# Cross-attention scores relative to the last key: 76 instead of 77 columns a head, heads interleaved key by key

## The chip, the cores and the metric

One core of one Trainium2 chip runs the whole kernel. The metric is the device time of one execution in microseconds, as the median of several runs.

## What is computed

A gated cross-attention layer with a linear layer behind it, over x of shape 4 x 2048 x 512 and a context of 4 x 77 x 384 (77 keys for each of 4 batches), with 16 heads of 64:

```
x = x + tanh(g_xattn) * attention(layernorm(x), ctx)
x = x + tanh(g_ffn) * (layernorm(x) @ W[idx] + b[idx])

q, k, v = xn @ Wq, ctx @ Wk, ctx @ Wv            # split into 16 heads of 64
sim  = einsum('bhid,bhjd->bhij', q, k) * 64**-0.5
attn = softmax(sim, axis=-1)                     # over the 77 keys j
out  = einsum('bhij,bhjd->bhid', attn, v) @ Wo + bo
```

A softmax doesn't change when the same number is taken from all scores of a row.

## The kernel before

**Folding.** Queries are never formed. In a first part (some 90 us) the kernel multiplies the projected keys by the turned Wq and the projected values by Wo, so that the scores of a row are x times a folded matrix, and the attention output is the probabilities times a folded matrix. `key_fold` makes the folded keys in 32 units (4 blocks of 128 features by 8 pairs of heads): two fp32 matmuls of B*J = 308 columns into a pair of PSUM banks. Each unit is then split into two f16 halves, high and low, in `a_split`: ScalarE casts the high half out of PSUM (`key_high`, L824), VectorE subtracts it for the low half (`key_low`, L1070). Seven units (`STAGED_KEYS`) take another way: ScalarE copies them to `k_stage` (L822), and GpSimd makes both halves from there (`key_split`, L660 and L662). `pair_of_heads` says where a unit's heads lie in `a_split`. Units of folded values, visited in turn with them (`VISITS`), go the same way through L811 and L1062. PSUM pairs are used in a round of four, so a matmul waits until the unit four places before it is out (`taken_before`).

**Projection.** `keys_of` (L1394) projects the keys: 24 fp32 matmuls of 308 columns from `ctxT`, the turned context that ScalarE copied out of PSUM (L741).

**Tiles.** Then 64 tiles of 128 rows of x run in a software pipeline; a loop body holds 8 tiles. For each tile TensorE issues:

- `scores` (L1355): 36 f16 matmuls. The 16 heads are laid into three PSUM banks of 6, 6 and 4 heads, of 462, 462 and 308 columns; each bank takes 4 blocks of features by 3 products (high x high, high x low, low x high), so 12 matmuls.
- products of the second layer (L1355 with 256 columns): 42 for two tiles.
- `attention` (L1355 with 512 columns, L1579): 29 matmuls for the tile before.

`s_bank` gives the bank: the scores rotate through banks 0 to 3, three a tile, and wait for the exponentials of the bank's last user. Behind the scores VectorE takes the maxima by head (`maxima`, L1151 and L1153), ScalarE 16 exponentials of 77 elements (`exponentials`, L858), VectorE multiplies by the reciprocal sums (L1162), ScalarE and VectorE split the probabilities into f16 halves (L873, L875, L425), SyncE issues their transposes by DMA (L564), and `attention` reads those in the next step. VectorE and ScalarE work strictly in the order of their `step` functions.

The first scores wait for the last folded units: `bank_folded(0)` for the low halves up to unit 29 (the last that used banks 0 and 1), `heads_folded(0)`, ahead of the last feature block of the first bank, for the staged units up to number 27.

## Time and profile before

| what | value |
|---|---|
| median of 3 runs | 1051.0 us (1050.85 to 1053.32) |
| profiled execution | 1052.3 us, span of its instructions 1050.5 us |
| TensorE matmul busy | 1034.4 us, 98% of the span |
| VectorE busy | 851.6 us, 81% |
| ScalarE busy | 743.7 us, 71% |
| GpSimd busy | 438.9 us, 42% |
| TensorE granted clock | 0.998 of full speed |

The span is from the first to the last instruction of the profiled execution. Busy time counts an engine's own work and not its waits; the chain that ended last is followed back from the last instruction, each time to what released it.

### The profile page before, as it was taken

To read this page: it belongs to the slowest core of one execution; us is meant where nothing else is said; L and a number is where in the kernel's file an instruction comes from. 1 tells how busy PE (TensorE), PEld (TensorE's weight loads), DVE (VectorE), ACT (ScalarE), POOL (GpSimd) and SP (SyncE) were. 2 spreads that over 40 slices of the span, in tenths; PEclk is the share of its full clock that TensorE was granted. 3 is DMA by queue.
4 is the path that set the end of the run, shared out by engine and by line. 5 is a ranking of instruction groups with operands and counts; after the bars stand their busy time and mean duration, and the time that the engine had idled before them with its cause. 6 is when DMAs were issued, how large, how long until landed. Compare 5 with 4: busy or idle time off the path is not lost.

```text
span 1050.5 us, 21819 instructions
## 1 busy us (share of the span) xinstructions
PE 1034.4 (98%) x6065; PEld 588.0 (56%) x6065; DVE 851.6 (81%) x1800; ACT 743.7 (71%) x2712; POOL 438.9 (42%) x635
## 2 busy tenths in 40 slices
PE   9998899999999999999999999999999999999998
PEld 7634455555555555555555555555555555555555
DVE  3867988888888887888888887888888887888876
ACT  3588887766776676767776677767776776767762
POOL 0575444444433343444433443444433443444322
PEclk9999999999999999999999999999999999999999
DMA  8413466656666656655666656655666656655655
GB/s 310 101 30 105 94 128 136 134 114 118 129 136 135 135 126 136 135 118 110 132 138 135 135 121 139 137 112 111 132 138 137 136 123 134 134 113 114 133 116 141
DMA packets 383639, 135.02 MB, mean 129 GB/s; under 512 B 361728, under 2 KB 363316, under 8 KB 383540
## 3 DMA queue, kind: packets, MB, share of 16 engines
q1 hardware_dynamic: 383476, 134.09, 59.0%
q14 instruction: 84, 0.69, 0.2%
q8 instruction: 15, 0.25, 0.1%
q0 software_dynamic: 64, 0.00, 0.0%
HBM read 27.48 MB, written 16.78 MB: 42 GB/s over the span
## 4 chain that ended last, share of the span: by engine, by line
PE 93%; DVE 3%; ACT 1%; DMA 1%; issue 1%; SPq 0%; POOL 0%; DVEq 0%
PE banks L1355 84%; PE banks L1579 3%; PE banks L1458 1%; PE banks L1385 1%; PE banks L1394 1%; PE banks L1466 1%; DVE vw_area L1062 1%; ACT vw_area L811 1%; PE banks L1447 1%; DMA fold_area<-in_ctx 1%; DMA work<-work 0%; ACT work L858 0%; DVE fold_area L1070 0%; DVE work L425 0%; DVE red L1153 0%
## 5 line engine op out<-in xcount | busy, mean ns | idle before, releaser
L858 ACT ACTIVATE work<-banks,red,cst 128x77 f32<-128x77 f32 x1024 | 409.1, 426 | 89.1 <-DVE red L1153 89.1
L1355 PE MATMUL banks<-fold_area,work 128*128 128x462 f16 (+1 forms) x2304 | 410.6, 336 | 1.4 <-DMA work<-work 0.7
L1355 PE MATMUL banks<-vw_area,work 128*128 128x512 f16 x1674 | 373.0, 380 | 2.6 <-DMA work<-work 2.6
L1355 PEld LDWEIGHTS banks<-fold_area,work 128*128 128x128 f16 x2304 | 223.9, 97 | 176.2 <-DMA work<-work 1.2
L1355 PEld LDWEIGHTS banks<-vw_area,work 128*128 128x128 f16 x1674 | 164.1, 98 | 188.4 <-DMA work<-work 2.9
L425 DVE SCALAR_TENSOR_TENSOR work<-work 128x256 f16<-128x256 f32 (+3 forms) x444 | 240.1, 575 | 3.8 <-ACT work L881 3.3
L858 ACT ACTIVATION_READ_ACCUMULATOR work<-banks,red,cst 128x1 f32 x1024 | 221.0, 216 | 0.0
L1151 DVE TENSOR_REDUCE stats<-banks 128x6 f32<-128x462 f32 (+1 forms) x192 | 112.0, 584 | 109.1 <-PE banks L1355 108.7
L1355 PE MATMUL banks<-work 128*128 128x256 f16 x1302 | 162.4, 272 | 1.6 <-DVE work L1236 1.6
L1355 PEld LDWEIGHTS banks<-work 128*128 128x128 f16 x1302 | 126.8, 98 | 33.1 <-DVE work L1236 2.2
L703 POOL TENSOR_TENSOR stats<-stats,cst 128x1 f32<-128x1 f32 x64 | 12.5, 195 | 283.8 <-DVE stats L1187 283.8
L873 ACT ACTIVATE work<-work 128x768 f16<-128x768 f32 (+1 forms) x128 | 82.0, 641 | 59.5 <-DVE work L1162 59.5
L624 POOL TENSOR_TENSOR stats<-stats,cst 128x1 f32<-128x1 f32 x64 | 50.1, 783 | 170.5 <-DVE stats L1006 170.5
L761 ACT ACTIVATE work<-work,stats 128x512 f32<-128x512 f32 x64 | 52.1, 814 | 94.0 <-POOL stats L629 79.1
L1162 DVE TENSOR_TENSOR work<-work,cst 128x924 f32<-128x924 f32 (+1 forms) x128 | 113.9, 890 | 4.4
L1236 DVE SCALAR_TENSOR_TENSOR work<-banks,cst,work 128x256 f32<-128x256 f32 x217 | 98.1, 475 | 22.6 <-issue 18.5
L727 POOL TENSOR_TENSOR work<-work 128x512 f32<-128x512 f32 x64 | 95.4, 1491 | 43.8 <-DVE work L1196 34.3
L881 ACT ACTIVATE work<-work 128x512 f16<-128x512 f32 x124 | 71.4, 576 | 9.6 <-DMA work<-work 5.9
L1153 DVE TENSOR_SCALAR red<-stats,cst 128x6 f32<-128x6 f32 (+1 forms) x192 | 60.8, 317 | 6.8
L1180 DVE SCALAR_TENSOR_TENSOR work<-banks,cst,work 128x512 f32<-128x512 f32 x64 | 47.6, 744 | 4.7 <-PE banks L1579 4.5
L721 POOL TENSOR_TENSOR work<-work 128x256 f32<-128x256 f32 x31 | 46.2, 1489 | 2.4
L1183 DVE BATCH_NORM_STATS2 stats<-work 128x6 f32<-128x512 f32 x64 | 44.5, 695 | 2.2
(145 smaller groups left out, 814.4 us busy)
## 6 DMA issues: line engine op xcount, KB each, us to landing
work<-in_x SPq DMA_DIRECT2D x64, 256.0 KB, 2.8
out<-work SPq DMA_DIRECT2D x63, 256.0 KB, 2.2
work<-work SPq DMA_TRANSPOSE x254, 3.1
fold_area<-in_L_xattn_Wo SPq DMA_DIRECT2D x4, 512.0 KB, 9.2
work<-in_L_ffn_W SPq DMA_DIRECT2D x2, 1024.0 KB, 7.0
fold_area<-in_L_xattn_Wq SPq DMA_DIRECT2D x2, 1024.0 KB, 12.9
fold_area<-in_L_xattn_Wk SPq DMA_DIRECT2D x2, 768.0 KB, 12.1
fold_area<-in_L_xattn_Wv SPq DMA_DIRECT2D x2, 384.0 KB, 6.8
```

What stands on the lines that cost most here:

```text
L425: return nc.vector.scalar_tensor_tensor(out=lo, in0=value, scalar=scale, in1=hi, op0=ALU.mult, op1=ALU.subtract)
L624: nc.gpsimd.tensor_tensor(ve1, mv1[:, 1:2], eps, ALU.add).then_inc(ve1_ready, 1)
L727: nc.gpsimd.tensor_tensor(xr[:, m2, :], xr[:, m2, :], bias, ALU.add).then_inc(x2b_ready, 1)
L761: nc.scalar.activation(xn_place(o1, m1), xr[:, m1, :], ACT.Identity, bias=nm1, scale=rstd1).then_inc(xn_ready, 1)
L858: nc.scalar.activation(probs_of(h, h + 1), s_bank(m, k)[:, (h - h0) * J:(h - h0 + 1) * J], ACT.Exp, bias=nmx[:, h:h + 1], scale=exp_scale, ...
L873: nc.scalar.activation(by_core(ps[:, h0 * CORE:h1 * CORE]), values[:, :, 0:CORE], ACT.Copy, scale=2.0 ** PROB_BITS).then_inc(p_hi, 1)
L881: nc.scalar.activation(group_stage(g)[:, 0, :], value, ACT.Copy, scale=2.0 ** XN_BITS).then_inc(x2_hi, 1)
L1151: nc.vector.reduce_max(mx[:, h0:h1], by_head(s_bank(m, k)), AX.X).then_inc(mx_ready, 1)
L1153: nc.vector.tensor_scalar(nmx[:, h0:h1], mx[:, h0:h1], nexp_scale, None, ALU.mult).then_inc(nmx_ready, 1)
L1162: nc.vector.tensor_tensor(values, values, factors.unsqueeze(2).to_broadcast([P, h1 - h0, J]), ALU.mult).then_inc(p_ready, 1)
L1236: nc.vector.scalar_tensor_tensor(out=half, in0=part, scalar=f_scale, in1=half, op0=ALU.mult, op1=ALU.add).then_inc(f_added, 1)
L1355: mm = nc.tensor.matmul(ps, lhs(l), rhs(r), start=first and n == 0, stop=last and n == 2, skip_group_check=onto)
```

## The change

The last key is made the zero of the scores. Four GpSimd subtractions (one per batch) make `ctxT_from_last`, the turned context of keys 0 to 75 less that of key 76; `keys_of` reads it, so projected and folded keys have 76 columns a batch and head (304 for 308), and a score is that of its key less that of the last. The values still use all 77 keys. In a bank of scores the columns are laid key by key, the bank's heads side by side: column j*6 + h (j*4 + h in the bank of four heads, which starts at column 152, so that all banks end at 456). TensorE writes 456 and 304 columns, in one stretch. Columns 456 to 461 of banks 0 to 3 stand for the last key: VectorE sets them to zero once, and TensorE never writes them again, since score matmuls end in front of them. The maxima and the exponentials read 77 elements of a head through `s_heads`, 6 (or 4) fp32 elements apart. `a_split` has the same order, so the fold writes f16 elements 6 (or 4) places apart.

```diff
+    JS = J - 1
+    HS = HEADS * JS
+    BS = B * JS
...
-        a_split = [fold_area[:, k * A_WORDS:(k + 1) * A_WORDS].bitcast(F16).rearrange("p (s b n) -> p s b n", s=2, b=B) for k in range(KT)]
+        a_split = [fold_area[:, k * A_WORDS:k * A_WORDS + B * HS].bitcast(F16).rearrange("p (s b n) -> p s b n", s=2, b=B) for k in range(KT)]
...
         def s_bank(m, k):
             h0, h1 = BANKS[k]
-            return banks[:, (3 * m + k) % S_BANKS, 0:(h1 - h0) * J]
+            return banks[:, (3 * m + k) % S_BANKS, HB * JS - (h1 - h0) * JS:HB * JS]
+        def s_heads(m, k):
+            h0, h1 = BANKS[k]
+            cols = banks[:, (3 * m + k) % S_BANKS, HB * JS - (h1 - h0) * JS:HB * JS + h1 - h0]
+            return cols.rearrange("p (j h) -> p h j", h=h1 - h0)
...
         def pair_of_heads(k, s, h):
             four, a = h // 2, h % 2
-            cols = a_split[k][:, s, :, 4 * four * J:4 * (four + 1) * J].rearrange("p b (e r j) -> p e b r j", e=2, r=2)
-            return cols[:, :, :, a, :]
+            cols = a_split[k][:, s]
+            if four == 1:
+                at, apart = HB - 2 + a, HB * JS - (HB - 2)
+                return cols[:, :, at:at + 2 * apart].rearrange("p b (e n) -> p e b n", e=2)[:, :, :, 0:HB * (JS - 1) + 1:HB]
+            n = (0, None, 1, 2)[four]
+            h0, h1 = BANKS[n]
+            pairs = cols[:, :, h0 * JS:h1 * JS].rearrange("p b (j i r) -> p i b r j", i=(h1 - h0) // 2, r=2)
+            first = (4 * four - h0) // 2
+            return pairs[:, first:first + 2, :, a, :]
...
+            for b in range(B):
+                keys = ctxT[:, :, b * J:(b + 1) * J]
+                pool.wait_ge(ctxT_copied, b + 1)
+                nc.gpsimd.tensor_tensor(ctxT_from_last[:, :, b * JS:(b + 1) * JS], keys[:, :, 0:JS], keys[:, :, JS:J].to_broadcast([P, CT, JS]),
+                                        ALU.subtract).then_inc(ctxT_shifted, 1)
...
-                    nc.scalar.activation(probs_of(h, h + 1), s_bank(m, k)[:, (h - h0) * J:(h - h0 + 1) * J], ACT.Exp,
+                    nc.scalar.activation(probs_of(h, h + 1), s_heads(m, k)[:, h - h0, :], ACT.Exp,
                                          bias=nmx[:, h:h + 1], scale=exp_scale, accum_out=sums[:, h:h + 1]).then_inc(exp_done, 1)
...
+                if (kind, n) == (KEY, UNITS - 3):
+                    assert all(pair_of(KEY, v) >= S_BANKS for v in (UNITS - 2, UNITS - 1))
+                    dve.wait_ge(k_staged, key_staged_before(UNITS))
+                    dve.wait_ge(a_lo, key_highs_after(UNITS - 3))
+                    nc.vector.memset(banks[:, 0:S_BANKS, HB * JS:HB * J], 0.0).then_inc(last_zeroed, 1)
...
-                nc.vector.reduce_max(mx[:, h0:h1], by_head(s_bank(m, k)), AX.X).then_inc(mx_ready, 1)
+                nc.vector.reduce_max(mx[:, h0:h1], s_heads(m, k), AX.X).then_inc(mx_ready, 1)
...
+                if h == 0:
+                    pe.wait_ge(ctxT_shifted, B)
...
                 for n, (h0, h1) in enumerate(BANKS):
+                    if is_tile(o, m, 0) and n == 0:
+                        pe.wait_ge(last_zeroed, 1)
...
                         mm = split_products(s_bank(m, n), lambda s: turned[:, s, k, :],
-                                            lambda s: a_split[k][:, s, m % B, h0 * J:h1 * J], k == LAST_FOLDED[0], k == LAST_FOLDED[-1])
+                                            lambda s: a_split[k][:, s, m % B, h0 * JS:h1 * JS], k == LAST_FOLDED[0], k == LAST_FOLDED[-1])
```

In `copy_k`, `key_high`, `pair_banks`, `keys_of` and `key_fold` the width 0:BJ becomes 0:BS; `kT` and `k_stage` shrink with it.

VectorE, at the end of the fold and into the first tile (L1070 in before, L1097 in the change, are the low halves of key units; names are output<-input tiles). Before:

```order
L1002 BN_STATS stats<-work 128x6
L1006 BN_AGGR stats<-stats 128x2
L1070 TENSOR_TENSOR fold_area<-banks,fold_area 128x2x4x77 x6
L425 SCALAR_TENSOR_TENSOR work<-work 128x512
L1151 TENSOR_REDUCE stats<-banks 128x6
```

The same place in the change:

```order
L1029 BN_STATS stats<-work 128x6
L1033 BN_AGGR stats<-stats 128x2
L1097 TENSOR_TENSOR fold_area<-banks,fold_area 128x2x4x76 x4
L1170 MEMSET banks 128x4x6
L1097 TENSOR_TENSOR fold_area<-banks,fold_area 128x2x4x76 x2
L446 SCALAR_TENSOR_TENSOR work<-work 128x512
L1183 TENSOR_REDUCE stats<-banks 128x6
```

The memset stands between the low halves of units 29 and 30; nothing else moved.

GpSimd, at its start (constants, then the zeroed pads of the value side, then the first value split). Before:

```order
L618 MEMSET cst 128x1
L631 MEMSET vw_area 128x32x8
L637 CAST vw_area<-work 128x4x208
```

In the change:

```order
L639 MEMSET cst 128x1
L655 TENSOR_TENSOR fold_area<-fold_area 128x3x76 x4
L658 MEMSET vw_area 128x32x8
L664 CAST vw_area<-work 128x4x208
```

The four subtractions stand ahead of the pads. TensorE's instructions keep their order and number; its score matmuls read 128x456 and 128x304 for 128x462 and 128x308.

## Rows read from the trace of the kernel before

**Rows 1.** The page: span, busy time, and the chain by engine.

```profile
span 1050.5 us, 21819 instructions
PE 1034.4 (98%) x6065; PEld 588.0 (56%) x6065; DVE 851.6 (81%) x1800; ACT 743.7 (71%) x2712; POOL 438.9 (42%) x635
...
PE 93%; DVE 3%; ACT 1%; DMA 1%; issue 1%; SPq 0%; POOL 0%; DVEq 0%
```

**Rows 2.** Busy time by stretch: PE, PEld, DVE, ACT, POOL, clock, DMA share, GB/s.

```profile
48.00:79.00 31.00, 28.16 (x199) 11.63 (x197) 21.59 (x30) 25.35 (x35) 23.97 (x25) 1.00 0.24 44
110.00:1020.00 910.00, 906.65 (x5238) 510.91 (x5236) 754.34 (x1629) 661.33 (x2529) 373.79 (x549) 1.00 0.61 128
```

**Rows 3.** The chain of waits in order of time: start, us, what.

```profile
23.15 3.11 PE banks L1394 x12
...
90.44 2.51 PE banks L1355 x12
...
115.54 4.90 DMA work<-work
...
184.43 14.70 PE banks L1355 x87
...
214.05 14.70 PE banks L1355 x87
...
1028.96 0.76 DVE work L1180
```

**Rows 4.** Groups by line and shape: busy us, mean ns, idle before.

```profile
L1355 PE MATMUL banks<-vw_area,work 128*128 128x512 f16 x1674 | 373.0, 380 | 2.6 <-DMA work<-work 2.6
L1355 PE MATMUL banks<-fold_area,work 128*128 128x462 f16 x1536 | 310.3, 358 | 1.4 <-DMA work<-work 0.7 <-issue 0.7
L1355 PE MATMUL banks<-fold_area,work 128*128 128x308 f16 x768 | 110.8, 294 | 0.0
L1151 DVE TENSOR_REDUCE stats<-banks 128x6 f32<-128x462 f32 x128 | 81.5, 637 | 96.8 <-PE banks L1355 96.4
L1151 DVE TENSOR_REDUCE stats<-banks 128x4 f32<-128x308 f32 x64 | 30.6, 478 | 12.3 <-PE banks L1355 12.3
L1070 DVE TENSOR_TENSOR fold_area<-banks,fold_area 128x616 f16<-128x616 f32 x25 | 19.0, 794 | 4.5 <-ACT fold_area L824 4.4
L824 ACT CAST fold_area<-banks 128x616 f16<-128x616 f32 x25 | 16.4, 688 | 0.7 <-PE banks L1466 0.7
L1062 DVE TENSOR_TENSOR vw_area<-banks,vw_area 128x1024 f16<-128x1024 f32 x11 | 13.4, 1222 | 7.4 <-ACT vw_area L811 7.4
L811 ACT CAST vw_area<-banks 128x1024 f16<-128x1024 f32 x11 | 11.1, 1012 | 4.6 <-PE banks L1458 4.5
L1153 DVE TENSOR_SCALAR red<-stats,cst 128x6 f32<-128x6 f32 x128 | 31.1, 243 | 4.5
L716 POOL TENSOR_TENSOR work<-work 128x256 f32<-128x256 f32 x31 | 37.5, 1210 | 2.4
```

**Rows 5.** Timeline: the start, and the end of the fold.

```profile
8.41 0.35 ACT L741 COPY fold_area<-banks 128x231 f32<-128x231 f32 x1 [1.22 <-PE banks L1375]
...
35.58 0.88 POOL L637 CAST vw_area<-work 128x832 f16<-128x832 f32 x1 [32.00 <-ACT work L795]
...
87.42 4.33 DVE L1070 TENSOR_TENSOR fold_area<-banks,fold_area 128x616 f16<-128x616 f32 x6
...
89.41 0.70 POOL L660 CAST fold_area<-work 128x616 f16<-128x616 f32 x1
90.19 1.31 POOL L662 TENSOR_TENSOR fold_area<-work,fold_area 128x616 f16<-128x616 f32 x1
90.44 12.67 PE L1355 MATMUL banks<-fold_area,work 128*128 128x462 f16 x72 [0.67 <-issue]
```

**Rows 6.** Timeline of one tile in the middle.

```profile
510.55 3.09 SPq L564 DMA_TRANSPOSE work<-work  x1
...
518.96 5.99 PE L1355 MATMUL banks<-vw_area,work 128*128 128x512 f16 x27
```

More of the change, by code:

```diff
@@ L93, in flamingo_layer @@
         ctxT = c.take(CT * BJ).rearrange("p (k n) -> p k n", k=CT)
+        ctxT_from_last = c.take(CT * BS).rearrange("p (k n) -> p k n", k=CT)
         assert c.at <= 3 * A_WORDS
@@ L153, in flamingo_layer @@
         c.at = folds
-        kT = c.take(HP * BJ).rearrange("p (h n) -> p h n", h=HP)
+        kT = c.take(HP * BS).rearrange("p (h n) -> p h n", h=HP)
         wqT = c.take(HP * D).rearrange("p (h n) -> p h n", h=HP)
-        k_stage = [c.take(2 * BJ).rearrange("p (e n) -> p e n", e=2),
-                   at(D + HP * BJ, 2 * BJ).rearrange("p (e n) -> p e n", e=2)]
-        assert c.at <= x2T_at and D + HP * BJ + 2 * BJ <= RING * D
+        k_stage = [c.take(2 * BS).rearrange("p (e n) -> p e n", e=2),
+                   at(D + HP * BJ, 2 * BS).rearrange("p (e n) -> p e n", e=2)]
+        assert c.at <= x2T_at and D + HP * BJ + 2 * BS <= RING * D
         free = x2T_at + KT * D
@@ L204, in flamingo_layer @@
             sem("ident_zero"), sem("ident_ready"), sem("floor_set"), sem("consts_set"), sem("pads_set"))
-        ctxT_done, ctxT_copied = sem("ctxT_done"), sem("ctxT_copied")
+        ctxT_done, ctxT_copied, ctxT_shifted = sem("ctxT_done"), sem("ctxT_copied"), sem("ctxT_shifted")
         v_done, v_copied, v_scaled, v_scaled_end = sem("v_done"), sem("v_copied"), sem("v_scaled"), sem("v_scaled_end")
@@ L231, in flamingo_layer @@
         s_done, mx_ready, nmx_ready, exp_done = sem("s_done"), sem("mx_ready"), sem("nmx_ready"), sem("exp_done")
+        last_zeroed = sem("last_zeroed")
         rsum_ready, p_ready, p_hi, p_lo, pT_turned, pad_zeroed = (
@@ L393, in pair_banks @@
         def pair_banks(first):
-            return banks[:, first:first + 2, 0:BJ].rearrange("p e (b j) -> p e b j", b=B)
+            return banks[:, first:first + 2, 0:BS].rearrange("p e (b j) -> p e b j", b=B)
         def pair_of_stage(stage):
@@ L777, in copy_k @@
                 nc.scalar.copy(kT[:, 2 * n:2 * n + 2, :],
-                               banks[:, pair_of(PROJECT, n):pair_of(PROJECT, n) + 2, 0:BJ]).then_inc(k_copied, 1)
+                               banks[:, pair_of(PROJECT, n):pair_of(PROJECT, n) + 2, 0:BS]).then_inc(k_copied, 1)
             copy_k(0)
@@ L821, in key_high @@
                         act.wait_ge(k_stage_lo, n - 1)
-                    nc.scalar.copy(k_stage[n % 2], banks[:, first:first + 2, 0:BJ]).then_inc(k_staged, 1)
+                    nc.scalar.copy(k_stage[n % 2], banks[:, first:first + 2, 0:BS]).then_inc(k_staged, 1)
                 else:
@@ L1393, in keys_of @@
                 for k in range(CT):
-                    mm = nc.tensor.matmul(banks[:, pair_of(PROJECT, h // 2) + h % 2, 0:BJ], wk_raw[:, k, h * P:(h + 1) * P], ctxT[:, k, :],
+                    mm = nc.tensor.matmul(banks[:, pair_of(PROJECT, h // 2) + h % 2, 0:BS], wk_raw[:, k, h * P:(h + 1) * P], ctxT_from_last[:, k, :],
                                           start=k == 0, stop=k == CT - 1)
@@ L1465, in key_fold @@
                     rows = slice(DH * e, DH * e + DH)
-                    nc.tensor.matmul(banks[:, pair_of(KEY, v) + e, 0:BJ], wqT[rows, h, k * P:(k + 1) * P], kT[rows, h, :],
+                    nc.tensor.matmul(banks[:, pair_of(KEY, v) + e, 0:BS], wqT[rows, h, k * P:(k + 1) * P], kT[rows, h, :],
                                      start=True, stop=True).then_inc(a_done, 1)
```

## The prediction

> **What bounds the kernel now.** I read the page first. TensorE is busy for 98% of the span and has 93% of the chain [rows 1]; the next engine, VectorE, is at 81%. An average can hide stages, so the second look is busy time by stretch: from 110 to 1020 us TensorE works 906.65 of 910 us, VectorE 754.34, ScalarE 661.33; in the fold (48 to 79 us) no engine is full, TensorE 28.16 of 31, ScalarE 25.35, GpSimd 23.97, VectorE 21.59 [rows 2]. The third is the chain in order of time: two tiles last 214.05 - 184.43 = 29.62 us, matmuls only, so 14.81 us a tile [rows 3]. The score matmuls waited 1.4 us in all, those of the attention 2.6 us [rows 4]. So what is taken from TensorE's stream in the steady part is taken from the time, unless another engine then falls behind.
>
> There are exceptions. From 90.44 us, where the first bank of the first tile starts, to the end of the DMA transpose at 115.54 + 4.90 = 120.44 us the chain runs through VectorE, ScalarE and that transpose [rows 3]; the scores of tiles 0, 1 and 2 are issued by then. At the end it leaves TensorE for VectorE at 1028.96 us, where the low halves of the last tile's probabilities are done in the same moment; of the last tile only the first bank lies ahead of both ways.
>
> **The price of a column.** A score matmul of 462 columns shows 358 ns and one of 308 shows 294 [rows 4]. The fixed part doesn't matter: (358 - 294) / 154 = 0.416 ns a column, which is one column a cycle at 2.4 GHz, the upper of the clock's two levels, granted throughout [rows 2]. The step from 462 to 512 columns gives (380 - 358) / 50 = 0.44, the same within rounding. All sizes here are in that linear range.
>
> **The sum, against the profiled execution (1052.3 us, of which 1050.5 are span).**
>
> 1. Scores. Per tile 24 matmuls lose 6 columns (2.5 ns each, 60 ns) and 12 lose 4 (1.66 ns each, 20 ns): 80 ns. 64 tiles less the first three and the last are 60, 60 x 0.080 = **-4.8 us**. The first bank counts in the first and last tile too: 2 x 12 x 2.5 ns = -0.06 us.
>
> 2. Projection and folds of the keys: 304 columns for 308, 608 elements for 616, 1.3% less. The projection lies on the chain (12 records take 3.11 us [rows 3], and there are 48, 12.4 us); about as much again of fold matmuls, casts and subtractions does. 1.3% of 25 us is **-0.3 us**.
>
> 3. The four subtractions on GpSimd. The nearest rows are its additions of 256 elements, up to 1210 ns [rows 4]: at most 4.8 us for four. The last piece of the turned context is ready at 8.41 + 0.35 = 8.76 us [rows 5], so they end by 14 us at the latest, and their reader, the key projection, starts at 23.15 us [rows 3]. Queued behind them are only the zeroed pads and the first split of the value side, which starts at 35.58 us after GpSimd has idled for 32.0 [rows 5]. Cost nothing, with 9 us of cover; without it up to 4.8 us.
>
> 4. The memset. The first scores start at 90.44 us, right behind the low half of unit 29: six low halves run from 87.42 for 4.33 us, 0.72 each, and the fourth (unit 29) ends at 90.3 [rows 5]. The memset must follow that one's completion, and TensorE now waits for it. Nothing of before shows a VectorE memset in PSUM. From below it is nothing; from above I take the small operation on 6 elements, 243 ns [rows 4], plus some 0.1 for the two handovers. I take **+0.2 us**, range 0 to 0.35. Behind it on VectorE stand the low halves of units 30 and 31, which only the last bank needs, 24 matmuls later. GpSimd isn't touched.
>
> 5. Steps of 12 bytes between f16 elements in SBUF (the fold), and of 24 or 16 bytes between fp32 elements in PSUM (maxima, exponentials). No row of before steps over single elements in this way. Rows give what a stream element costs: VectorE (1222 - 794) / 408 = 1.05 ns, ScalarE (1012 - 688) / 408 = 0.79 ns, the maxima (637 - 478) / 154 = 1.03 ns [rows 4]. So they move one element a cycle or nearly, and with one element at a time being moved, packing buys nothing that a step could lose. I take **0**, and a second cycle per element as the other end, priced in the rivals.
>
> Sum: -4.8 - 0.06 - 0.3 + 0.2 = -5.0 us. The profiled execution would take 1047.3 us. It was 1.3 us above the median of the runs, so the median goes from 1051.0 to **1046.0 us**, 0.48% less.
>
> **Rivals.**
>
> A. *A stepped read of PSUM costs a second cycle per element.* Then each maximum over 6 heads takes 462 x 1.03 = 0.48 us more and that over 4 heads 0.32, 1.27 us a tile on VectorE; each exponential takes 77 x 0.79 = 61 ns more, 0.98 us a tile on ScalarE. In the steady part both fit: VectorE works 754.34 / 910 x 14.81 = 12.3 us a tile and would work 13.5 of 14.73, ScalarE 10.8 and then 11.7 [rows 2]. The probabilities would be later by some 0.48 + 0.98 = 1.5 us, and have the room: their transpose is issued at 510.55 us and takes 3.09, while the attention that reads it starts at 518.96, 5.3 us later [rows 6]. It shows only where the chain leaves TensorE: 1.5 us in tile 0, 1.3 in tile 1, 1.5 in the last, 4.3 us together, so 1046.0 + 4.3 = 1050.3 us, no change to be measured. For it: nothing in the trace; against it: that these reads already go one element at a time. The Trainium skill speaks for it: "Advanced Engine Details and Errata", section Memory Cachelines, gives PSUM lines of two fp32 values and says that each two consecutive elements should be contiguous for best throughput, which these reads never are; its sentence on a significant slowdown speaks of matmuls, whose writes here stay contiguous. By that rule the time would be this rival's; no run here shows it yet.
>
> B. *A stepped access of SBUF costs a second cycle per f16 element; the slower side.* Place: the 25 units of the fold that ScalarE casts and VectorE subtracts. A cast would take 616 x 0.79 = 0.49 us more, a low half 0.65. The last eight units run close behind one another on VectorE, 8 x 0.65 = 5.2 us on the path. In the 17 before, which alternate with value units, ScalarE has 31 - 25.35 = 5.65 us free and would need 17 x 0.49 = 8.3, so at least 2.7 us; at most all 17 x 0.65 = 11 us. In all 7.9 to 16.2, say 12: 1046.0 + 12 = 1058.0 us. It gives the whole gain and 0.3% back from 8.2 us on, 0.33 us a unit. Against it: these casts and subtractions already move one element at a time, no faster into f16 than the maxima read fp32 [rows 4].
>
> C. *Only GpSimd pays for the step.* Its seven splits write by steps and read the high half back by steps. The last (unit 25) ends at 90.19 + 1.31 = 91.50 us [rows 5], and the first bank needs it after 9 of its 12 matmuls, at 90.44 + 0.75 x 2.51 = 92.3 [rows 3]: 0.8 us to spare. If both operations of the last two splits doubled (2.0 us each), the scores would be 3.2 us late: 1049.2 us at most; if the subtraction alone took half as much again, 2 x 0.66 - 0.8 = 0.5 us, 1046.5. The second is what a page says: the Trainium skill, "GPSIMD Engine Reference", section Performance pitfalls for Q7 kernels, states that reads of SBUF with steps over 8 bytes take 50% longer. It was measured on another kind of code; no row here shows it yet.
>
> That the change doesn't shorten TensorE's stream at all isn't open: the shapes stand in the instructions, and the price per column in the rows.
>
> **How the numbers follow.** The forecast has 0.75; A 0.10, B 0.07, C 0.08 (in between, mostly near the forecast). The range holds the forecast with its bounds (the two small gains up to twice as large, the memset 0 to 0.35, half a microsecond for the median of a few runs) and most of C: 1044.8 to 1048.6. A and B are left out with 0.17. A measurement of this kernel tells some 0.3%, 3.2 us, from no change, so "faster" ends at 1047.8: forecast 0.73 of its 0.75 and C 0.06, 0.79. "Same": A 0.10, and the rest of C and of the forecast, 0.13. "Slower": B and what isn't thought of, 0.08.
>
> **What would show it.** Right: the score matmuls show 358 - 2.5 = 355.5 and 294 - 1.7 = 292.3 ns; two tiles last 29.62 - 0.16 = 29.46 us in the chain; the first scores start at about 90.4 us (0.3 earlier, 0.2 later); the maxima keep 637 and 478 ns, the exponentials their mean duration, the casts and low halves of the fold 688 and 794 less 1.3%. Wrong: maxima near 1100 ns (A), low halves near 1400 ns and first scores after 98 us (B), GpSimd's subtraction near 2 us and a wait of TensorE within the first bank (C). The forecast itself would be wrong if two tiles still last 29.6 us, which would mean that matmuls aren't paid by columns, or if the attention began to wait for its transposes.

## The result: 3.3% slower, and the profile after

The change takes 1086.1 us (median of 4 runs, 1085.1 to 1088.4) against 1051.0 us before: ratio 1.0328, 95% interval 1.0308 to 1.0348. The prediction, 1046.0 us in a range of 1044.8 to 1048.6, was wrong by 40 us, and the change makes the kernel slower where a gain was forecast. The profiled execution took 1088.4 us, of which 1086.6 are span.

The page of the change: span, busy time, granted clock by slice, chain by engine and by group (compare [rows 1]).

```profile
span 1086.6 us, 21826 instructions
PE 1045.2 (96%) x6065; PEld 591.7 (54%) x6065; DVE 882.3 (81%) x1801; ACT 775.6 (71%) x2712; POOL 454.8 (42%) x639
PEclk9968799999999999999999999999999999999999
PE 87%; DVE 6%; ACT 4%; DMA 2%; issue 1%; SPq 0%; POOL 0%; DVEq 0%
PE banks L1387 79%; DVE fold_area L1097 3%; PE banks L1615 2%; ACT fold_area L851 2%; ACT work L885 1%; PE banks L1417 1%; PE banks L1428 1%; PE banks L1492 1%; PE banks L1500 1%; DMA fold_area<-in_L_xattn_Wv 1%; PE banks L1481 1%; DMA work<-work 1%; DVE work L446 1%; DVE vw_area L1089 0%; DVE work L1194 0%
```

ScalarE and VectorE are busy some 31 us longer, and the low halves and casts of the fold (L1097 and L851, in before L1070 and L824) have a place in the chain that they didn't have. The clock falls in slices 3 to 5, which is 54 to 136 us.

The groups by line and shape of the change, to be held against [rows 4]:

```profile
L1387 PE MATMUL banks<-fold_area,work 128*128 128x456 f16 x1536 | 307.8, 358 | 3.9 <-DVE banks L1170 3.0 <-DMA work<-work 0.8
L1387 PE MATMUL banks<-fold_area,work 128*128 128x304 f16 x768 | 109.7, 293 | 0.0
L1183 DVE TENSOR_REDUCE stats<-banks 128x6 f32<-128x462 f32 x128 | 81.5, 637 | 93.4 <-PE banks L1387 93.2
L885 ACT ACTIVATE work<-banks,red,cst 128x77 f32<-128x77 f32 x1024 | 408.9, 425 | 87.4 <-DVE red L1185 87.3
L1097 DVE TENSOR_TENSOR fold_area<-banks,fold_area 128x608 f16<-128x608 f32 x25 | 50.5, 2078 | 17.1 <-ACT fold_area L851 16.9
L851 ACT CAST fold_area<-banks 128x608 f16<-128x608 f32 x25 | 49.8, 2140 | 5.5 <-PE banks L1500 5.4
L687 POOL CAST fold_area<-work 128x608 f16<-128x608 f32 x7 | 14.2, 2034 | 14.2 <-ACT work L849 14.2
L689 POOL TENSOR_TENSOR fold_area<-work,fold_area 128x608 f16<-128x608 f32 x7 | 14.4, 2063 | 0.6
L655 POOL TENSOR_TENSOR fold_area<-fold_area 128x228 f32<-128x228 f32 x4 | 2.1, 563 | 2.9 <-ACT fold_area L768 2.9
```

The matmuls of 456 columns show 358 ns in the mean, as those of 462 did, and not the 355.5 of the forecast; but up to 140 us this mean holds 46 records of 399 ns from a stretch at a lower clock, and in the versions below whose fold is fast and whose columns lie well the same shape shows 356. The maxima keep 637 ns although they read PSUM 24 bytes apart. The cast goes from 688 to 2140 ns, the low half from 794 to 2078, GpSimd's cast to 2034. Packed, the three engines needed 1.1 to 1.3 ns an element (688, 794 and GpSimd's 700 over 616); now the casts need 3.3 to 3.5, whichever engine makes them. So it isn't the engine's own pace that is paid.

The means mix two steps. Units in a bank of six heads write 12 bytes apart, those in the bank of four heads 8 bytes, and the low halves take some 2.2 and 1.5 us; the timeline has both kinds:

```profile
113.91 1.50 DVE L1097 TENSOR_TENSOR fold_area<-banks,fold_area 128x608 f16<-128x608 f32 x1
...
116.09 2.25 DVE L1097 TENSOR_TENSOR fold_area<-banks,fold_area 128x608 f16<-128x608 f32 x1 [0.69 <-ACT fold_area L851]
```

Busy time by stretch; the first row is the stretch of [rows 2], the others go on to the first maxima:

```profile
48.00:79.00 31.00, 22.76 (x134) 10.81 (x135) 19.70 (x15) 24.28 (x20) 20.15 (x18) 0.72 0.30 52
79.00:94.00 15.00, 10.21 (x56) 3.20 (x54) 13.30 (x14) 13.48 (x12) 9.48 (x6) 0.89 0.00 1
94.00:110.00 16.00, 11.44 (x62) 2.99 (x60) 12.43 (x8) 14.54 (x11) 12.36 (x9) 0.79 0.00 1
110.00:132.00 22.00, 13.75 (x53) 5.97 (x54) 19.34 (x15) 18.43 (x14) 10.77 (x11) 0.69 0.24 72
```

From 48 to 79 us VectorE gets 15 instructions done for 30, ScalarE 20 for 35, and TensorE 134 matmuls for 199. Then VectorE is busy for 45.1 of 53 us. In the chain of waits the fold ends so:

```profile
116.92 2.25 ACT fold_area L851
...
119.19 8.48 DVE fold_area L1097 x4
...
127.99 4.10 PE banks L1387 x12
...
132.12 0.65 DVE stats L1183
...
414.56 13.96 PE banks L1387 x81
```

**Where 36.1 us of span went.** Figures of single moments are each from one profiled execution. The first maxima start at 132.12 us (in before at 90.44 + 2.51 and a handover, 92.98): +39.1. From there to those of the last tile 919.0 us pass, in before 924.6: -5.5, 4.8 of it in the 60 tiles of the forecast. From there to the end 35.45 us for 32.95: +2.5. The steady part did what was forecast, the fold took seven times as much, and the tail took half of the gain back.

### The profile page after: what moved, and what is told of

It is laid out like the page before. It is cut to its first block, busy times and chain, and to the rows that moved or that the text cites. A ratio compares the mean times of both kernels' runs of the same rounds, so it can differ in the third digit from the quotient of the medians.

```text
span 1086.6 us, 21826 instructions
## 1 busy us (share of the span) xinstructions
PE 1045.2 (96%) x6065; PEld 591.7 (54%) x6065; DVE 882.3 (81%) x1801; ACT 775.6 (71%) x2712; POOL 454.8 (42%) x639
## 4 chain that ended last, share of the span: by engine, by line
PE 87%; DVE 6%; ACT 4%; DMA 2%; issue 1%; SPq 0%; POOL 0%; DVEq 0%
PE banks L1387 79%; DVE fold_area L1097 3%; PE banks L1615 2%; ACT fold_area L851 2%; ACT work L885 1%; PE banks L1417 1%; PE banks L1428 1%; PE banks L1492 1%; PE banks L1500 1%; DMA fold_area<-in_L_xattn_Wv 1%; PE banks L1481 1%; DMA work<-work 1%; DVE work L446 1%; DVE vw_area L1089 0%; DVE work L1194 0%
## 5 line engine op out<-in xcount | busy, mean ns | idle before, releaser
L1387 PE MATMUL banks<-fold_area,work 128*128 128x456 f16 (+1 forms) x2304 | 406.8, 336 | 3.9 <-DVE banks L1170 3.0
L1097 DVE TENSOR_TENSOR fold_area<-banks,fold_area 128x608 f16<-128x608 f32 x25 | 50.5, 2078 | 17.1 <-ACT fold_area L851 16.9
L851 ACT CAST fold_area<-banks 128x608 f16<-128x608 f32 x25 | 49.8, 2140 | 5.5 <-PE banks L1500 5.4
```

Of the source, the lines that this page charges most:

```text
L851: nc.scalar.copy(pair_of_heads(k, 0, h), pair_banks(first)).then_inc(a_hi, 1)
L1097: nc.vector.tensor_tensor(pair_of_heads(k, 1, h), pair_banks(pair_of(KEY, v)), pair_of_heads(k, 0, h), ALU.subtract).then_inc(a_lo, 1)
L1387: mm = nc.tensor.matmul(ps, lhs(l), rhs(r), start=first and n == 0, stop=last and n == 2, skip_group_check=onto)
```

## Experiments

K is "the key projection, GpSimd's subtractions, the memset or the waits for them", W is "writing f16 by steps". Two figures are read from every trace: when the first maxima start (the fold's end) and how long two tiles last. Each experiment was timed in one of three rounds, beside fresh executions of the kernel before (medians 1052.3, 1051.8 and 1052.4 us), and its ratio is to those of its own round. Between versions with a fast fold the first maxima come anywhere from 91.4 to 95.8 us, so a microsecond or two at that place says nothing.

### The order of columns alone

Before, with its 77 keys and nothing else of the change (of `pair_of_heads` only the main case is shown):

```diff
 def pair_of_heads(k, s, h):
-    cols = a_split[k][:, s, :, 4 * four * J:4 * (four + 1) * J].rearrange("p b (e r j) -> p e b r j", e=2, r=2)
-    return cols[:, :, :, a, :]
...
+    pairs = cols[:, :, h0 * J:h1 * J].rearrange("p b (j i r) -> p i b r j", i=(h1 - h0) // 2, r=2)
...
-    nc.vector.reduce_max(mx[:, h0:h1], by_head(s_bank(m, k)), AX.X)
+    nc.vector.reduce_max(mx[:, h0:h1], s_heads(m, k), AX.X)
```

> All 77 keys, no last-key zero: only the order of columns is that of the change (heads side by side, key by key) in a_split and in the banks. Theory W (writing f16 elements 12 or 8 bytes apart in SBUF is what costs, whatever the engine): the casts of the fold take some 2150 ns and the subtractions some 2090 as in the change, the first maxima come near 132 us, two tiles last 29.62 us as before, and the time is that of the change plus what 61 to 63 tiles gained there, 1086 + 5 = 1091 us. Rival K (the key differences, the narrower matmuls or the memset cost it, the order of columns being free): casts stay at 688 ns and the time at 1051 us.

1087.1 us, ratio 1.0346 (1.0306 to 1.0386):

```profile
L1080 DVE TENSOR_TENSOR fold_area<-banks,fold_area 128x616 f16<-128x616 f32 x25 | 50.9, 2098 | 15.8 <-ACT fold_area L834 15.8
L834 ACT CAST fold_area<-banks 128x616 f16<-128x616 f32 x25 | 50.9, 2147 | 5.4 <-PE banks L1476 5.3
L1161 DVE TENSOR_REDUCE stats<-banks 128x6 f32<-128x462 f32 x128 | 81.4, 636 | 96.5 <-PE banks L1365 96.0
```

Without any of K's parts the first maxima come at 128.5 us: 35.5 of the 39.1 us are the order of the columns. Two tiles last 29.62 us, as before. Of the other 3.6 us, 2.0 arise ahead of the fold: the key projection started later in the change's trace (25.04 for 23.05 us, with 2.6 us of waiting for a DMA of Wv, which this trace doesn't have). The rest comes in the middle of the fold, where 152 matmuls took 30.7 us at a mean clock of 0.76 in the change (54 to 97 us) and 27.1 at 0.88 here (52 to 94 us). It doesn't come from the memset: TensorE's wait ahead of the first scores is 2.8 us here, without one, and 3.0 in the change. The time forecast for this version was 1091 us; it came out 4 us lower. The forecast had put the whole gain of the change's tiles on top, of which its tail, as said above, gives 2.5 us back; the rest is less than the four executions differ by (1084.9 to 1095.1 us).

### The last key off, heads apart

The change without its interleaving; the bank gets runs of 76 columns 77 apart, the hole between them is the zero (the fold, the readers and the memset follow the same places):

```diff
 def s_bank(m, k):
-    return banks[:, (3 * m + k) % S_BANKS, HB * JS - (h1 - h0) * JS:HB * JS]
+    return banks[:, (3 * m + k) % S_BANKS, 0:(h1 - h0) * J].rearrange("p (h j) -> p h j", j=J)[:, :, 0:JS]
```

> Last key taken off as in the change, but heads stay one behind the other: the fold writes runs of 76 f16 elements, a score matmul writes 6 (or 4) runs of 76 columns with a hole of one between them, and the six holes of a bank hold the zeros; maxima and exponentials read packed. Theory W: casts at 680 ns and subtractions at 785 ns, first maxima at 92.5 to 93.5 us, two tiles in 29.46 us, so 1046 us: the gain that was forecast for the change. Rival P (TensorE pays for an output in several runs): two tiles last longer than 29.6 us and the 4.8 us are not there, 1051 us or more. Rival K: 1085 us as in the change.

1052.8 us, ratio 1.0005 (0.9989 to 1.0021): rival P of the expectation. The casts take 673 ns, the low halves 784, the first maxima come at 92.3 us: K is out, since all its parts are in this kernel, and the fold is as fast as before. But two tiles last 29.61 us and the matmuls show 360 and 296 ns: the six and four columns that aren't written are paid all the same (what they are paid for comes below). Loss and gain of the change both hang on how the columns are laid, the gain on the side of TensorE's output.

### TensorE does the interleaving

Heads apart in SBUF, packed interleaved in the bank; TensorE reads its moving operand 152 bytes apart:

```diff
-    lambda s: a_split[k][:, s, m % B, h0 * JS:h1 * JS]
+    lambda s: a_split[k][:, s, m % B, h0 * JS:h1 * JS].rearrange("p (h j) -> p j h", j=JS)
```

> Banks, maxima and exponentials as in the change, but a_split keeps a head's 76 columns together, and the score matmuls read their moving operand by steps of 152 bytes to bring it into the bank's order. Theory W: the fold is as fast as before (first maxima at 93 us). If TensorE reads a stepped operand at one column a cycle, the time is 1046 us as for the hole; if each column then costs a second cycle, a tile takes 36 x 0.17 = 6.2 us more and the time is near 1046 + 64 x 6.2 = 1440 us; neither price is in any trace so far.

2387.5 us. A matmul of 456 columns shows 979 ns for 358, one of 304 shows 692, with the granted clock at 0.64 in the steady part although TensorE is busy for all of it. Both figures of the expectation, 1046 and 1440 us, missed it. The fold is as fast as before: the first scores start at 89.2 us, and the first maxima come at 99.0 only because the matmuls ahead of them are so long. How much of the 979 ns is the step and how much the clock isn't separated: in the 10 us from 510 us, which hold none but stepped matmuls, the granted clock is 0.50, the lower of its two levels (1.2 GHz), and from 530 to 540 us, where the others run, it is 0.98. Together they cost TensorE 0.62 us for a matmul of six heads and 0.40 for one of four, in every tile.

### What a step costs, by itself

Behind the last tile of before, single operations on packed fp32 sources that write f16 or fp32 at a growing step, or read f16 by steps; first on three engines at once, then one engine after another (one profiled execution of each, and each operation timed two or three times in it):

```diff
+    out_ = (area.bitcast(F16) if width == 2 else area)[:, 0:count * step].rearrange("p (n s) -> p n s", s=step)[:, :, 0]
+    write(out_, probs[:, 0:count]).then_inc(probe[n], 1)
```

> The kernel before, with measurements behind the last tile: on each of ScalarE, VectorE and GpSimd, writes of 600 + (step in bytes) elements from packed fp32 into f16 at steps of 2, 4, 6, 8, 12 and 16 bytes and into fp32 at steps of 4, 8, 12 and 16 bytes, and reads of 300 + (step in bytes) f16 elements at steps of 2, 4, 8, 12 and 16 bytes written packed; three times each. The time of the kernel means nothing. Theory W1 (a 2-byte write without its neighbour costs, whatever the step): f16 at 4 bytes is already as slow as at 12, some 2100 ns, and fp32 at 12 bytes is as fast as packed, some 700. Theory W2 (the step costs, whatever the size): f16 and fp32 at 12 bytes are both near 2100 ns, and the time grows with the step. Theory R (the stepped read of the high half costs too): reads at 12 bytes are slower than packed ones by more than their extra elements. VectorE and GpSimd: the same order.

> The kernel before, and behind its last tile single operations one after another, now one engine at a time (ScalarE, then VectorE, then GpSimd, two passes): writes of some 600 elements (some 200 above 16-byte steps) from packed fp32 into f16 at steps of 2, 4, 6, 8, 12, 16, 24, 32, 48 bytes and fp32 at 4, 8, 12, 16, 32; then f16 reads at 2 to 16. The time of the whole means nothing. If the price belongs to each engine's own write, ScalarE shows the durations of the first probe, f16 689, 872, 1210, 1552, 2251, 2948 ns, and VectorE and GpSimd now rise evenly too, to 2000 to 2400 ns at 12 bytes. If engines share the port that writes, alone they are well below: ScalarE under 1500 ns at 12 bytes. If the price is a line touched per element, it stops growing past a step: at 32 and 48 bytes the price per element is that of 16 (about 4.8 ns); if it is the stretch of memory passed over, it grows to about 9 and 13 ns.

ScalarE alone; the element count tells the step (601 is packed, 602 is 4 bytes apart, 603 6, 604 8, 606 12, 608 16; 192 is 24, 204 is 48):

```profile
L988 ACT CAST fold_area<-work 128x601 f16<-128x601 f32 x1 | 0.7, 697 | 0.0
L988 ACT CAST fold_area<-work 128x602 f16<-128x602 f32 x1 | 0.9, 862 | 0.0
L988 ACT CAST fold_area<-work 128x603 f16<-128x603 f32 x2 | 2.4, 1202 | 0.1
L988 ACT CAST fold_area<-work 128x604 f16<-128x604 f32 x2 | 3.1, 1538 | 0.1
L988 ACT CAST fold_area<-work 128x606 f16<-128x606 f32 x2 | 4.4, 2214 | 0.1
L988 ACT CAST fold_area<-work 128x608 f16<-128x608 f32 x2 | 5.8, 2878 | 0.1
L988 ACT CAST fold_area<-work 128x192 f16<-128x192 f32 x2 | 2.1, 1030 | 0.1
L988 ACT CAST fold_area<-work 128x204 f16<-128x204 f32 x2 | 2.3, 1126 | 0.1
```

| bytes from element to element | 2 | 4 | 6 | 8 | 12 | 16 |
|---|---|---|---|---|---|---|
| f16 write of some 605, ScalarE, ns | 697 | 862 | 1202 | 1538 | 2214 | 2878 |
| VectorE | 790 | 828 | 1164 | 1500 | 2168 | 2852 |
| GpSimd | 687 | 852 | 1184 | 1522 | 2192 | 2872 |
| fp32 write of some 605, ScalarE | | 693 | | 728 | 992 | 1258 |
| f16 read of some 305, ScalarE | 443 | 444 | | 462 | 604 | 745 |

In the table the step of 2 bytes is the packed f16 write, 4 bytes the packed fp32 one. From 4 bytes on the f16 duration grows evenly, (2878 - 862) / 12 / 605 = 0.28 ns an element and byte of step, and from 16 bytes on it stays at some 5 ns an element (1030 / 192 = 5.4 at 24 bytes, 1126 / 204 = 5.5 at 48, with the fixed part of one instruction). The same holds on all three engines within 50 ns from 4 bytes on. So it is as if each 16 bytes of SBUF that a write touches cost some 4.7 ns with f16 elements and 2 with fp32, whether one element or several fall in them; packed f16 hides it behind the engine's own pace. Reads show it from 8 bytes on, with less than half the price. That answers the expectations. A missing neighbour isn't the price (4 bytes cost 872 ns in the first probe and not 2100), but nor is the step alone, whatever the size of the element (fp32 at 12 bytes takes 1024 ns and not 2100). The engines don't share the cost either: alone, ScalarE needs 2214 ns at 12 bytes, where under 1500 was expected of a shared port. And the price stops growing at 16 bytes, as it would for lines touched. With the three engines at once ScalarE's durations were the same to 5% (2251 at 12 bytes), VectorE's uneven (1433 for a packed write, 2418 at 12). The Trainium skill, "Advanced Engine Details and Errata", section Memory Cachelines, gives SBUF 16-byte lines and says that at least two hits on a line are needed to absorb the access: the size of 16 bytes agrees with where the growth ends here, but steps of 6 and 8 bytes, which hit a line twice or more, already cost 1.7 and 2.2 times the packed write.

By this table a write of some 605 elements takes VectorE 2.17 us at 12 bytes and 1.50 at 8, and the two kinds of low halves in the change show some 2.2 and 1.5. The means of the fold, 2.08 to 2.15 us, are the mixture.

### Two heads side by side

The dose, that is, the same cause at a smaller step: before with pairs of heads interleaved, so that the fold writes f16 4 bytes apart for 12.

```diff
-    cols = a_split[k][:, s, :, 4 * four * J:4 * (four + 1) * J].rearrange("p b (e r j) -> p e b r j", e=2, r=2)
+    cols = a_split[k][:, s, :, 4 * four * J:4 * (four + 1) * J].rearrange("p b (e j r) -> p e b r j", e=2, r=2)
```

> The kernel before (77 keys) with one edit: two heads side by side instead of six, so f16 writes of the fold step 4 bytes instead of 12, and the maxima and exponentials read PSUM at 8-byte steps. If the cost of a write grows with its step (the probe: ScalarE f16 689 ns packed, 872 at 4 bytes, 2251 at 12), a cast takes about 880 ns and a low half about 950, ScalarE needs 25 x 0.2 = 5 us more against some 5.6 us of slack, and the first maxima come at 93 to 97 us: 1051 to 1055. If any step over single elements costs the full price (casts 2100 ns), it is the change's fold again: first maxima 128 us, 1087. Matmuls and the two tiles' 29.62 us don't change in either.

1052.7 us, ratio 0.9998 (0.9984 to 1.0013). A cast takes 893 ns and a low half 884, and the first maxima come at 92.5 us, no later than before: 0.2 us a unit vanishes in the slack of [rows 2] (ScalarE is now busy for 27.20 of the 31 us, TensorE for 27.69), while 1.45 us a unit cost 35.5. The price is that of the write's step, and only what exceeds the slack is paid.

### What TensorE pays for a hole

Heads 80 apart in the bank (holes of 4), then 78 apart (holes of 2), for 77, in the writes as in the reads:

```diff
-    ...rearrange("p (h j) -> p h j", j=J)[:, :, 0:JS]
+    ...rearrange("p (h j) -> p h j", j=80)[:, :, 0:JS]
```

> Edit, from the hole version: heads stand 80 columns apart in the bank instead of 77, so the hole behind each head's 76 columns is 4 wide and not 1; as many columns written, as many holes. If a hole costs TensorE one column whatever its width (a restart per stretch), nothing changes: two tiles 29.61 us, 1052.8 us. If it is the distance in the bank that is paid, each of the 24 matmuls of six heads loses 18 more columns x 0.416 = 7.5 ns and each of the 12 of four heads 5 ns, 0.24 us a tile: two tiles 30.09 us, 1068 us. The maxima and exponentials keep 637, 478 and 425 ns in both.

> Edit, from the version with heads 77 columns apart (the 1-column hole, two tiles 29.61 us): 78 apart, so that each head's 76 columns start at an even column (8 bytes) but only every second one at a multiple of 4 (16 bytes). If TensorE pays for each pair of columns that a stretch touches (at 77 apart three of six heads start odd and touch 39 pairs for 38: 6 columns of a matmul of six heads, 4 of one of four, just what was measured), two tiles last 29.45 us as at 80 apart, intervals 192.5 and 129 ns, and the time is that of 80 apart, 1050.7. If it pays for each 4 columns touched, three of six and two of four heads cost 4 columns more: two tiles 29.45 + 0.32 = 29.77 us, 1060.

Both theories of the first were wrong: the wider holes cost less. The chain of waits in the middle of the run, 77 apart, 80 and 78 apart (start, us, what):

```profile
406.57 14.04 PE banks L1379 x81
421.05 14.70 PE banks L1379 x87
```

```profile
408.95 13.96 PE banks L1379 x81
423.35 14.62 PE banks L1379 x87
```

```profile
405.71 13.96 PE banks L1379 x81
420.11 14.62 PE banks L1379 x87
```

The same 87 instructions take 0.08 us less, the whole 80 ns a tile of the forecast, with every hole in place. So in these three versions a hole is free, and it is the start at an odd column that costs: at 77 apart three of six heads (two of four) start odd, and 76 columns from an odd start touch 39 pairs of columns for 38, which makes 6 (and 4) columns, just what was lost. At 78 all heads start at 8 bytes but not at 16, and nothing is lost either, so the unit is a pair. The Trainium skill, "Advanced Engine Details and Errata", section Memory Cachelines, gives PSUM lines of 8 bytes, with which this agrees; that any non-contiguous pattern slows matmuls significantly, as it says too, these writes don't show. In the change the maxima and exponentials read PSUM 24 bytes apart at their old pace.

80 apart gives 1050.7 us, ratio 0.9976 (0.9959 to 0.9992), 78 apart 1049.9 us, ratio 0.9974 (0.9961 to 0.9988): faster than before, but by some 2.5 us and not by 5.

### The rest of the gain: the tail

The tail is the time from the last tile's first maxima to the end. It takes 35.7 us in the version with 80, about as in the change (35.45), and 32.95 in before. The timeline of the version with 80 there:

```profile
1027.26 0.82 PE L1379 MATMUL banks<-work 128*128 128x256 f16 x6
...
1029.57 0.83 PE L1379 MATMUL banks<-work 128*128 128x256 f16 x6 [1.48 <-DVE work L1260]
...
1031.16 4.45 PE L1590 MATMUL banks<-vw_area,fold_area 128*128 128x512 f16 x12 [0.77 <-DMA fold_area<-work]
```

The same place in before, where the attention follows without a wait:

```profile
1030.89 0.83 PE L1355 MATMUL banks<-work 128*128 128x256 f16 x6 [1.30 <-DVE work L1236]
...
1031.55 2.75 PE L1562 MATMUL banks<-vw_area,fold_area 128*128 128x512 f16 x12
```

And by stretch, first this version, then before:

```profile
1028.00:1032.00 4.00, 1.75 (x11) 0.95 (x11) 3.26 (x7) 1.85 (x3) 1.13 (x2) 0.97 0.91 198
1032.00:1036.00 4.00, 4.00 (x13) 1.46 (x12) 0.82 (x2) 0.14 (x1) 1.27 (x1) 0.60 0.81 110
```

```profile
1028.00:1032.00 4.00, 2.70 (x20) 1.59 (x18) 3.42 (x9) 1.61 (x3) 0.92 (x2) 1.00 0.91 193
1032.00:1036.00 4.00, 4.00 (x20) 1.83 (x19) 1.90 (x3) 0.63 (x1) 1.43 (x2) 1.00 0.81 133
```

TensorE arrives sooner, waits twice, 2.25 us in all where before waits 1.30 once, and then the granted clock is 0.60 for a stretch: 12 matmuls take 4.45 us for 2.75. Waits (0.95 us more) and clock (1.70) make up 2.65 of the 2.75 us by which the tail is longer. The change shows the same (waits of 1.49 and 0.56 us, 12 matmuls 4.45), and so does the version 78 apart (1.48, 0.69, 4.45). The version 77 apart, whose stream is as long as before's, waits once, for 1.30 us, and its clock holds; its tail is 34.0 us all the same, with a wait of 0.51 us for VectorE further on. The test moves work into the second wait, here and in before as its control:

```diff
 product(*pair, 0)
+product(*pair, 1)
 attention(*last)
-product(*pair, 1)
```

> Edit, from the version with heads 80 columns apart in the bank: in TensorE's last steps product 1 of the last pair (6 matmuls, 0.83 us) stands ahead of the attention of the last tile instead of behind it. In the version it comes from, TensorE idles 1.48 and 0.77 us around 6 matmuls at 1028 us, waiting for VectorE and then for the transposes of the last probabilities; the next 12 matmuls take 4.45 us where the kernel before has 2.59, with the granted clock at 0.60 in that stretch, and from tile 63's first maxima to the end it is 35.7 us against 32.95 of before. If that idle time is what the shorter stream turned into and what takes the clock down, the second wait is filled, the 12 matmuls take 2.6 us, the tail is about 33.0 us and the time 2.5 us below the version's 1050.7: 1048.2, ratio 0.995. If the clock falls all the same, only 0.8 us is won: 1050. If the tail is bound by something else, 1050.7.

> The kernel before with the same one edit in TensorE's last steps (product 1 ahead of the last attention), as the control of that experiment. In before the single wait of 1.30 us lies ahead of product 0, the attention then starts without a wait and the clock holds. If the tail's loss belongs to the shorter stream, nothing is to be had here: 1051, within 0.1%, perhaps 0.8 us slower, since the last attention comes 0.83 us later. If the order is better in itself, this is faster by 1 us or more too, and the gain of the other run is no evidence on the 76 columns.

With 80 apart: 1048.3 us, ratio 0.9969 (0.9953 to 0.9985). The second wait is 0.26 us, and the clock holds:

```profile
1023.93 1.48 PE L1379 MATMUL banks<-work 128*128 128x256 f16 x12 [1.48 <-DVE work L1260]
1025.67 2.76 PE L1590 MATMUL banks<-vw_area,fold_area 128*128 128x512 f16 x12 [0.26 <-DMA fold_area<-work]
```

The tail takes 34.2 us, 1.5 less where 2.7 were expected. The control says why: in before the same edit gives 1052.7 us, ratio 1.0003 (0.9990 to 1.0016), and a tail of 34.15 us for 32.95. There the order costs 1.2 us: the last attention starts 0.7 us later, and behind it TensorE waits 0.83 us for VectorE. By difference the edit saves 2.7 us where the clock would fall; 2.2 of them can be read off, 1.69 from the matmuls and 0.51 from the wait.

With the second wait filled the clock held, so in these traces its fall in the tail came with the idle time ahead of it. That is read from one execution of each version. Of the twelve executions with the edit three show a mean clock of 1.0 and three 0.995; of the ten without it none shows 1.0 and five 0.995 or less. As times the versions can't be told apart: 0.9969, 0.9974 and 0.9976 have intervals that overlap. All three are 0.2 to 0.3% below before.

### Packed, without a zero column

Heads 76 apart with no place for the last key: nmx is capped at 0, one small exponential a bank puts exp(nmx) into the 77th place, and VectorE adds it to the sums.

```diff
+    nc.scalar.activation(by_head(probs_of(h0, h1))[:, :, JS], nmx[:, h0:h1], ACT.Exp).then_inc(last_exp, 1)
...
+    nc.vector.tensor_tensor(sums[:, h0:h1], sums[:, h0:h1], values[:, :, JS], ALU.add).then_inc(last_added, 1)
```

> Edit, from the hole version (last key off, heads apart in SBUF): the 76 columns of a head now stand packed in the bank, with no place for the last key, so TensorE writes 456 and 304 columns in one stretch and there is no memset. The last key's score is zero by construction: nmx becomes min(-scale x maximum, 0), its probability exp(nmx) is one small ScalarE operation a bank into the 77th place of each head, and VectorE adds it to the sums before the reciprocal, twice a tile. If the matmuls are paid by the columns written in one stretch (the change's own steady part: 29.45 us for two tiles) and the fold is fast as in the hole version (first maxima 92.3 us), two tiles last 29.46 us, casts 675 and low halves 785 ns, first maxima about 92, and the time is 1051.0 - 4.8 - 0.3 + about 0.6 for the small operations where the chain leaves TensorE = 1046.5 us, ratio 0.996. If the small operations cost TensorE a wait in every tile (probabilities late), two tiles last over 29.6 us and the time is 1051 or more. If the gain in the steady part hangs on something else in the change than the stretch, 1051.5.

1054.0 us, ratio 1.0014 (0.9999 to 1.0029): no gain. Single pairs of tiles do last 29.45 us, but a pass of the loop (8 tiles) takes 118.5 us as before and not 117.8. From 110 to 1020 us, this version and then the one with 80 apart:

```profile
110.00:1020.00 910.00, 902.79 (x5227) 509.60 (x5226) 804.93 (x1748) 677.06 (x2717) 364.16 (x548) 1.00 0.61 127
```

```profile
110.00:1020.00 910.00, 906.03 (x5263) 514.27 (x5261) 758.21 (x1635) 665.66 (x2550) 375.28 (x552) 1.00 0.61 128
```

VectorE has 46.7 us more, 0.76 us a tile. At each return of the loop it stands still for some 3.2 us, and the loss lies there: three tiles round the return take 14.7 to 14.9, 15.2 to 15.4 and 14.4 to 14.6 us where the version with 80 apart has 14.4, 15.05 and 14.4, and the other five keep that version's pace. What causes it is shown only in part. TensorE waits for VectorE ahead of a product at four of the returns (0.33 us at 299 us, then 0.26, 0.16 and 0.20), which is at most half of the 0.7 us a pass; the rest I haven't resolved. (That TensorE is busy for 3.2 us less in the stretch is no measure of it: 1.8 of them are longer waits for DMA, most at the first tiles.) VectorE had room for the additions in the mean; the loop's return is where the mean doesn't hold.

## Why the prediction was wrong, by its steps

1. *Scores, -4.8 us.* Right: the same instructions last 0.08 us less a tile, and 117.8 for 118.48 us in a pass of the loop. The price of a column held: two tiles last 29.45 us where 29.46 were forecast.
2. *Projection and folds, -0.3 us.* Hidden under step 5 in the change; in the version 77 apart the fold's end is at 92.3 for 93.0 us, but in the other versions with a fast fold, with 76 columns or with 77, it moves from 91.4 to 95.8. So the runs can't show this term.
3. *GpSimd's subtractions, 0.* Right: four of 563 ns for up to 1210, done by 8.3 us, long before the projection.
4. *The memset, +0.2 us.* Right. It took 78 ns, below the 243 taken as its upper end. TensorE waits in front of the first scores with a memset or without one, since they stand behind the low half of unit 29 in either case: 0.67 us in before [rows 5] and 0.89 in the version 77 apart, 2.82 in the version with the order of columns alone and 3.03 in the change, 0.2 us more each time.

```profile
124.48 6.74 PE L1365 MATMUL banks<-fold_area,work 128*128 128x462 f16 x27 [2.82 <-issue]
```

```profile
89.72 6.61 PE L1379 MATMUL banks<-fold_area,work 128*128 128x456 f16 x37 [0.89 <-DVE banks L1162]
```

5. *Steps, 0.* **This is the step that failed.** Its two halves came out differently: the stepped reads of PSUM cost nothing (rival A is out), the stepped f16 writes of SBUF cost 1.45 us a cast and 1.28 a low half. The argument was that an engine that moves one element at a time gains nothing from packing and so can't lose it. That looks at the engine's pace only. The 0.79 and 1.05 ns an element of [rows 4] come from packed writes, and say nothing of a limit behind them that packed f16 writes stay below. Three engines of different pace met the same one, each by itself; that it lies in the memory and not on the way to it isn't shown.

Rival B had the place, the units, the slack of 5.65 us and the sign, with a chance of 0.07 and a price of "a second cycle": 0.49 us for a cast where 1.45 was measured, 0.65 for a low half where 1.28 was. By its own working the measured price gives 8 x 1.28 = 10.2 us for the last units and 17 x 1.45 - 5.65 = 19.0 for the 17 before, 29.2 of 35.5 us; the rest may be the clock, which fell to 0.72 in the starved fold (the fold's matmuls show 577 ns for 449 in a fast fold; in the chain of the version with the order alone four of them take 1.45 us, where eight take 1.50 in before). How much of this lies on the path wasn't worked out. That a second cycle bounded the cost from above was an assumption without a row: with no row of a stepped write, its upper end was open, and a range that left this case out wholly was too narrow.

Rival C is out as the cause, since all three engines pay. GpSimd pays as they do, and for the write above all: its cast, which only writes by steps, goes from 698 to 2034 ns, its subtraction, which reads by steps too, from 1317 to 2063. In the probe its stepped f16 read takes 910 ns at 12 bytes for 754 packed. Its last split ends at 124.8 us, ahead of the first scores, and TensorE doesn't wait within the first bank.

Not in the prediction at all: the tail. I had read the end of the chain as TensorE's or as equal to it, and counted the whole gain of 60 tiles. It comes back 2.5 to 2.75 us short, because the end waits for a chain through VectorE, ScalarE and the transposes that the columns don't shorten, and because the clock falls behind the longer wait (12 matmuls take 1.70 us more). Even with a free fold the change would have given only some 2.5 to 3 us, an estimate from its own 5.5 less 2.5 and from the versions 78 and 80 apart.

## What to carry to other kernels

A new access pattern has a price on each side that touches it, and a packed duration bounds none of them: before a layout is chosen, a few single operations at its step, on the engine and element size concerned, settle what no row of the trace holds. If a layout must be paid somewhere, pay it in fp32 reads of PSUM, which were free here, not in f16 writes of SBUF, and for TensorE's output start each run at an even column rather than close the holes. Before a wait is put down to a new instruction, compare it with the wait at the same place without that instruction. And where an engine's stream gets shorter, look at the one place that it waits already: there the gain turns into idle time, and perhaps into a lower clock.

## What the runs showed that I had not expected

- f16 writes into SBUF: 0.28 ns an element and byte of step up to 16 bytes, then flat, the same on ScalarE, VectorE and GpSimd.
- fp32 writes into SBUF pay less for the same step: 992 ns at 12 bytes for 693 packed, 1258 at 16, where f16 needs 2214 and 2878.
- Maxima and exponentials read fp32 from PSUM at 24-byte steps in 637 and 425 ns, no more than packed.
- Matmul output in runs of 76 columns costs nothing for the holes if each run starts at an even column (78 and 80 apart), and one more pair of columns for a run that starts at an odd one (77 apart).
- A moving operand read at 152-byte steps takes 979 ns for 358, with the granted clock at 0.64 in the mean of the steady part.
- In the tail TensorE waited 1.48 us, ran six matmuls, waited 0.77 us, and its clock fell, to 0.60 in the mean of the next 4 us (12 matmuls 4.45 us for 2.75); after the one wait of 1.30 us in before it held.

Left open: why f16 costs twice as much as fp32 for the same 16 bytes, and where between the engines and the memory the price arises. VectorE's standstill of 3 us at the loop's return is in all versions, and its cause is open.
